# Windowed attention products over 64 keys, in one array shape of 64 rows by 32 columns

## The chip, the cores and the metric

The kernel runs on one core of one Trainium2 chip. The metric is the device time of one execution in microseconds (us), median of three runs. All times of instructions come from one profiled execution of the kernel before.

## What is computed

Eight batches of 512 tokens with 128 features are normalised, and two things are added to them: a global attention with 16 heads of width 8, and a stack of six layers. Each layer is a windowed attention followed by a gated feed-forward part. The windowed attention has 16 heads of width 64 and windows of 32 tokens; a query sees the 64 keys of its own window and of the one before it.

```
for i in range(DEPTH):                                     # 6 layers
    x = attn_layer(shift_tokens(x), Wqkv[i], q_scale[i], k_scale[i], Wo[i]) + x
    x = ffn_layer(shift_tokens(x), ln_g[i], ln_b[i], W1[i], b1[i], W2[i], b2[i]) + x
...
sim = jnp.einsum('bhwie,bhwje->bhwij', bq, bk2) * QK_SCALE # 32 queries x 64 keys, head width 64
sim = jnp.where(mask, -jnp.finfo(sim.dtype).max, sim)
attn = jax.nn.softmax(sim, -1)
out = jnp.einsum('bhwij,bhwje->bhwie', attn, bv2)
```

## The kernel before

Four blocks follow each other: the layer norm, the global attention, the windowed stack, and the final addition. The change concerns the windowed stack, `windowed_stack`, and the constants and buffers it takes from `Early`.

The stack works on 48 units, one for each layer and batch, of 512 tokens, which are four tiles of 128 tokens. Every engine runs a list of stages written out by hand (`PE_ORDER`, `DVE_ORDER`, `ACT_ORDER`, `POOL_ORDER`, `SP_ORDER`), again and again; a name such as `s2` is the stage `s` of tile 2, and a dash behind it says that it belongs to the unit before, so that two units overlap. Semaphores tie the stages together; nothing is reordered. TensorE's list, once a unit, is

```
q0 k0 qT3- kT3- r2- s3- vb2- k1 va2- kT0 q1 qT0 v0 r3- k2 va3- vb3- s0 q2 wo- qT1 r0 v1 kT1 centre- vb0 va0
var- q3 v2 s1 k3 qT2 h0- kT2 h1- r1 h2- s2 vb1 v3 va1 y-
```

`q`, `k`, `v` are the projections of a tile (line 1072); VectorE rotates q and k out of PSUM (`rotate_q`, `rotate_k`), ScalarE and GpSimd make the norms, VectorE scales (`scale_q`, `scale_k`), and TensorE transposes the result (`qT`, `kT`, line 1023), which ScalarE copies out. `s` makes the scores of a tile: two bf16 products lay the mask into both PSUM banks of a slot (line 1030), and 64 fp32 products of 32 queries by 64 keys are added to it (line 1041). VectorE takes the maximum and subtracts it, ScalarE takes the exponential (`exp`), `r` transposes the probabilities, ScalarE copies them to `probT`. `probT` holds in its 128 partitions the 64 keys of two windows, one above the other.

`va` and `vb` multiply the probabilities with the values (line 1053). Each of these stages has 16 fp32 products with 128 rows (two windows' keys) and 130 columns: the value buffers `va` and `vb` hold for each head two copies of 65 columns (64 values and a one, for the sum), of which one has zeros where the keys of the other window lie, so that one product gives both windows' results side by side. The second buffer, `vb`, holds the values shifted down by one window; the SyncE queue makes it from `va` with four DMAs a tile. ScalarE writes a tile of `va` with two copies of 64 partitions (lines 945 and 946). VectorE divides the results (lines 886 and 887) and transposes them (`turn`), and `wo` projects them (line 1095). `centre`, `var`, `h`, `y` are the feed-forward part.

PSUM is four slots of two banks. A stage on TensorE waits until the engine that read the stage before in its slot is done (`SLOTS_OF`). In TensorE's program the first four units are written out, then a loop goes over the rest, four units a turn; its head is aligned by `eng.addr_align(FETCH)`. A `passed` is a semaphore increment of the engine to itself; it stands behind some waits.

Of the kernel before, what the change touches and what calls it, by code (L numbers as in the profile page):

```python
# [6 lines left out]
BF16 = mybir.dt.bfloat16  # L7
# [33 lines left out]
class Early:  # L41

    def __init__(self, nc, ctx):
        sb = lambda n, s, d=F32: ctx.enter_context(nc.sbuf_tensor(n, s, d))
        sem = lambda n: ctx.enter_context(nc.semaphore(n))
        self.w_qkv = sb("w_qkv", [P, 2, 3, INNER])
        self.w_o = sb("w_o", [P, QCH, D])
        self.w_1 = sb("w_1", [P, 2, NJ, JW])
        self.w_2 = sb("w_2", [JW, NJ, D])
        self.b_1 = sb("b_1", [JW, 2, NJ])  # L50
        self.vec = sb("vec", [P, 3])
        self.qks = sb("qks", [P, 2, 2, DH])
        self.rot = sb("rot", [P, TPB, 4, DH])
        self.pair16 = sb("pair16", [P, 2, DH], BF16)
        self.mask = sb("mask", [P, 2, SEQ], BF16)
        self.ones = sb("ones", [P, P])
        self.centring = sb("centring", [P, P])
        self.zero = sb("zero", [P, 1])
        self.epsc = sb("epsc", [P, 1])
        self.least = sb("least", [P, 1])  # L60
        self.minus_least = sb("minus_least", [P, 1])
        self.xs = sb("xs", [P, SEQ])
        self.xs2 = sb("xs2", [P, SEQ])
        self.kT = [sb(f"kT{i}", [P, QCH, WIN + P]) for i in range(2)]
        self.va = sb("va", [P, VTILES, 2, HEADS, VA])
        self.vb = sb("vb", [P, VTILES, 2, HEADS, VA])
        self.S = {n: sem("ws_" + n) for n in ("const_loaded", "const_ready", "w_q", "w_k", "w_v", "qks_loaded", "w_ff",
                                              "cleared", "mask_loaded", "kept", "fetched")}

# [23 lines left out]
def layer_norm_and_transpose(nc, io, res, xT, ident, early):  # L93

    with ExitStack() as ctx:
# [30 lines left out]
        @block.gpsimd  # L126
        def _(pool):
            cleared, ready = early.S["cleared"], early.S["const_ready"]
            for k in early.kT:
                pool.memset(k[:, :, :], 0.0).then_inc(cleared, 1)  # L130
            for buffer, value in ((early.ones, 1.0 / D), (early.zero, 0.0), (early.epsc, EPS), (early.least, 1e-24),
                                  (early.minus_least, -1e-24), (early.xs, 0.0), (early.xs2, 0.0)):
                pool.memset(buffer[:, :], value).then_inc(cleared, 1)
            for v in (early.va, early.vb):
                pool.memset(v[:, :, :, :, :], 0.0).then_inc(cleared, 1)
            pool.wait_ge(cleared, 11)
            pool.wait_ge(loaded, 32)
            nc.gpsimd.tensor_tensor(early.centring[:, :], ident[:, :], early.ones[:, :], ALU.subtract).then_inc(cleared, 1)
            pool.wait_ge(cleared, 12)
            for v in (early.va, early.vb):  # L140
                pool.memset(v[0:DH, :, 0, :, DH:VA], 1.0).then_inc(ready, 1)
                pool.memset(v[DH:P, :, 1, :, DH:VA], 1.0).then_inc(ready, 1)

        @block.vector
        def _(dve):
# [22 lines left out]
        @block.scalar  # L168
        def _(act):
            act.wait_ge(agg_done, TILES + 1)  # L170
            nc.scalar.activation(std[:, :], std[:, :], ACT.Sqrt).then_inc(std_done, 1)
            for b in range(BATCH):
                act.wait_ge(transposed, b + 1)
                nc.scalar.copy(xT[:, b, :], ps[b % 2][:, :]).then_inc(moved, 1)
            act.wait_ge(early.S["mask_loaded"], 16)
            nc.scalar.copy(early.mask[:, :, :], mask32[:, :, :]).then_inc(early.S["const_ready"], 1)
            act.wait_ge(loaded, 32)
            for r in range(2):
                rows = slice(DH * r, DH * r + DH)
                nc.scalar.copy(early.pair16[rows, :, :], ident[rows, None, rows].broadcast_to([DH, 2, DH])).then_inc(  # L180
                    early.S["const_ready"], 1)

        @block.tensor
# [448 lines left out]
def windowed_stack(nc, io, xT, ident, early):  # L632
# [5 lines left out]
    with ExitStack() as ctx:  # L638
# [8 lines left out]
        qks = early.qks  # L647
        rot = early.rot
        table = sb("table", [P, TPB, 4, DH])
        pair16 = early.pair16  # L650
        mask = early.mask
        ones = early.ones
        centring = early.centring
# [32 lines left out]
                                                        "rstd_link", "passed"]}  # L686
        S.update(early.S)
        vb_ready = [sem(f"ws_vb_ready{t}") for t in range(TPB)]
        VB_DMAS = [3] + [4] * (TPB - 1)
        W_FF = 5  # L690
        CONSTS = 7
        block = ctx.enter_context(nc.Block())

        wait = event_wait(S, EVENTS)
# [59 lines left out]
        @block.sync  # L754
        def _(sp):
            for t in range(TPB):
                sp.sem_inc(vb_ready[t], 16 * VB_DMAS[t])
            def layer_end(it, l):

                for kind in "qkv":  # L760
                    wait(sp, kind + "_filled", it, 0)
                    passed(sp)
                sp.wait_ge(S["tables"], l + 1)
                passed(sp)
                early.load_qkv(sp, io, (l + 1) % DEPTH, (l + 1) % 2)
                if not isinstance(l, int):

                    wait(sp, "y_read", it - 1)
                    early.load_ff(sp, io, l)

            def stage(kind, t, unit, batch, before, starts, layer):

                s = t % VTILES
                wait(sp, "v_read", unit, t)
                sp.dma_start(vb[32:64, s, 0, :, :], va[0:32, s, 0, :, :]).then_inc(vb_ready[t], 16)
                sp.dma_start(vb[64:96, s, 1, :, :], va[32:64, s, 0, :, :]).then_inc(vb_ready[t], 16)
                sp.dma_start(vb[96:128, s, 1, :, :], va[64:96, s, 1, :, :]).then_inc(vb_ready[t], 16)
                if t:
                    sp.dma_start(vb[0:32, s, 0, :, :], va[96:128, (t - 1) % VTILES, 1, :, :]).then_inc(vb_ready[t], 16)
            units(sp, SP_ORDER, stage, layer_end)  # L780

            for name in ("w_q", "w_k", "w_v", "qks_loaded"):
                sp.wait_ge(S[name], 16 * (DEPTH + 1))
            for kind in "qkv":
                wait(sp, kind + "_filled", DEPTH * BATCH - 1, TPB - 1)
            early.fetch(sp, io)
# [21 lines left out]
        def _(dve):  # L808
# [39 lines left out]
            def stage(kind, n, unit, batch, before, starts, layer):  # L848
# [31 lines left out]
                elif kind in ("va", "vb"):  # L880
# [1 line left out]
                    wait(dve, kind + "_filled", unit, n)  # L882

                    wait_tile(dve, "turned", unit, n)
                    ps = slot(kind, n)[:, :, 0:4 * PITCH].rearrange("p r (w d) -> p r w d", d=PITCH)
                    link(nc.vector.reciprocal(rden[:, a], ps[:, :, :, DH]), kind)
                    nc.vector.tensor_tensor(o[:, a].rearrange("p w r d -> p r w d"), ps[:, :, :, 0:DH],  # L887
                                            rden[:, a, :, :, None].broadcast_to([P, 2, 4, DH]), ALU.mult).then_inc(S[kind + "_read"], 1)
                elif kind == "turn":

# [26 lines left out]
        def _(act):  # L917
# [9 lines left out]
            def stage(kind, n, unit, batch, before, starts, layer):  # L927
# [7 lines left out]
                elif kind == "v":  # L935
# [6 lines left out]
                        wait_vb(act, unit_of, old + 1)  # L942
                    wait(act, "v_filled", unit, n)
                    ps = flat("v", n).rearrange("p (h d) -> p h d", d=DH)
                    nc.scalar.copy(va[0:DH, n % VTILES, 0, :, 0:DH], ps[0:DH])  # L945
                    nc.scalar.copy(va[DH:P, n % VTILES, 1, :, 0:DH], ps[DH:P]).then_inc(S["v_read"], 1)
                elif kind == "qT":
                    wait(act, "qT_filled", unit, n)

# [67 lines left out]
        def _(pe):  # L1017
# [6 lines left out]
                return last  # L1024

            def scores(t):
                for r in range(2):
                    rows = slice(DH * r, DH * r + DH)

                    nc.tensor.matmul(slot("s", t)[:, r, :], pair16[rows, :, :].rearrange("p a n -> p (a n)"),  # L1030
                                     mask[rows, 0 if t == 0 else 1, :],
                                     start=True, stop=False, skip_group_check=True)
                for a in range(2):
                    for n, w in enumerate(WINDOWS):
                        tok = WIN * w
# [10 lines left out]

            def products(kind, t):
                a = ("va", "vb").index(kind)
                for r in range(2):
                    for n, values in enumerate((vb, va)):  # L1050
                        for g in range(4):

                            last = nc.tensor.matmul(  # L1053
                                slot(kind, t)[32 * g:32 * g + 32, r, 0:4 * PITCH].rearrange("p (w d) -> p w d", d=PITCH)[
                                    :, n::2, 0:VA],
                                probT[:, 4 * r + 2 * a + n, 32 * g:32 * g + 32],
                                values[:, t % VTILES, :, 2 * (4 * a + g) + r, :],
                                start=True, stop=True, skip_group_check=True)
                return last

            def stage(kind, n, unit, batch, before, starts, layer):
# [15 lines left out]
                elif kind == "s":  # L1077
                    wait(pe, "qT_read", unit, n)
                    wait(pe, "kT_read", unit, n)
                    last = scores(n)  # L1080
                elif kind == "r":
                    wait(pe, "probs", unit, n)
# [143 lines left out]
```

## Time and profile before

| | |
|---|---|
| median of three runs | 3814.31 us (3814.22 to 3814.42) |
| span of the profiled execution, first to last instruction | 3806.1 us |
| of it: layer norm and global attention | 473.5 us |
| of it: windowed stack and final addition, 48 units | 3332.6 us |
| mean granted TensorE clock | 0.984 of full speed |

The span is 8.2 us (0.2%) less than the median of the runs. Busy shares are those of the whole span. "PE" is TensorE's matrix products, "PEld" its weight loads, which run beside them. An fp32 product appears as two weight loads and two MATMULs, a bf16 product and a transpose as one of each.

### The profile page before, as it was taken

The numbers are of one execution on the slowest core, as the hardware profiler recorded it, in microseconds if no ns is written. First come the engines' busy times: TensorE is split into PE (matmuls) and PEld (weight loads), VectorE is DVE, ScalarE is ACT, GpSimd is POOL, SyncE is SP. The second block draws the span as 40 slices with busy tenths as digits, with TensorE's granted clock in tenths as the row PEclk, the third lists the DMA queues.
The fourth block names the chain that finished last, engine by engine and source line by source line (L and its number), as shares of the span: only waits on it lengthen the run. The fifth ranks groups of instructions, "written<-read, shape, count | busy, mean of one in ns | idle before, by whom it ended". The sixth has DMA issues, their size and how long they took to land. (4 is left out here: it accounts for less than half of the span.)

```text
span 3806.1 us, 123350 instructions
## 1 busy us (share of the span) xinstructions
PE 3546.5 (93%) x51360; PEld 2001.1 (53%) x51360; DVE 3233.6 (85%) x3696; ACT 2526.1 (66%) x3409; POOL 1558.0 (41%) x926
## 2 busy tenths in 40 slices
PE   5999879899999999999999999999999999999997
PEld 2333245555555555555555555555555555555554
DVE  7999778788888888888888888888888889888895
ACT  4888757667666666666766667667666666666764
POOL 4333144344434444434444434344444434444341
PEclk7999989999999999999999999999999999999999
DMA  2000011111121111121111111111211111211112
GB/s 69 2 1 1 23 44 34 28 27 34 29 61 34 27 34 28 37 58 27 34 28 34 50 38 34 28 29 38 55 34 29 27 40 27 62 29 27 37 30 62
DMA packets 60833, 130.63 MB, mean 34 GB/s; under 512 B 16004, under 2 KB 31880, under 8 KB 60424
## 3 DMA queue, kind: packets, MB, share of 16 engines
q1 hardware_dynamic: 60424, 124.06, 13.4%
q8 instruction: 393, 6.44, 0.7%
q14 instruction: 16, 0.13, 0.0%
HBM read 23.58 MB, written 4.19 MB: 7 GB/s over the span
## 5 line engine op out<-in xcount | busy, mean ns | idle before, releaser
L798 POOL TENSOR_TENSOR half_sq<-sq 128x1024 f32<-128x1024 f32 x192 | 500.9, 2609 | 1541.9 <-ACT sq L933 1531.9
L1072 PE MATMUL slot<-w_qkv,xs 128*128 (+1 forms) x2304 | 1102.7, 608 | 25.6 <-issue 17.3
L803 POOL TENSOR_TENSOR cosq<-cosq,sinq 128x1024 f32<-128x1024 f32 x384 | 902.2, 2366 | 368.7 <-DVE sinq L843 368.7
L933 ACT ACTIVATE sq<-slot 128x1024 f32<-128x1024 f32 x384 | 392.0, 1021 | 405.3 <-PE slot L1072 405.3
L1072 PEld LDWEIGHTS slot<-w_qkv,xs 128*128 128x128 f32 x2304 | 411.2, 192 | 432.2 <-issue 423.5
L841 DVE TENSOR_TENSOR cosq<-slot,table 128x1024 f32<-128x1024 f32 x384 | 467.7, 1218 | 143.4 <-ACT sq L933 133.1
L869 DVE TENSOR_TENSOR qk<-cosq,ry 128x1024 f32<-128x1024 f32 x384 | 517.8, 1359 | 11.6 <-ACT ry L990 9.5
L843 DVE TENSOR_TENSOR sinq<-slot,table 128x1024 f32<-128x1024 f32 x384 | 465.8, 1213 | 0.0
L1023 PEld LDWEIGHTS slot<-ident,qk 128*128 128x128 f32 x3072 | 349.5, 141 | 215.0 <-issue 125.3
L1023 PE MATMUL slot<-ident,qk 128*128 128x128 f32 x3072 | 396.1, 275 | 36.4 <-DVE qk L869 32.2
L1053 PE MATMUL slot<-vb,probT 128*32 128x130 f32 x6144 | 327.7, 280 | 16.9 <-issue 10.6
L1095 PE MATMUL slot<-oT,w_o 128*128 128x512 f32 x768 | 339.2, 595 | 2.4 <-DVE oT L894 2.4
L1041 PE MATMUL slot<-kT,qT 64*32 64x64 f32 x24576 | 296.2, 226 | 47.9 <-issue 47.3
L1053 PE MATMUL slot<-va,probT 128*32 128x130 f32 x6144 | 324.1, 276 | 14.6 <-issue 14.6
L455 DVE TENSOR_REDUCE at_rowmax<-at_slot 128x2 f32<-128x1024 f32 x256 | 303.9, 1219 | 14.6 <-PE at_slot L550 14.2
L1041 PEld LDWEIGHTS slot<-kT,qT 64*32 64x32 f32 x24576 | 258.2, 105 | 98.1 <-issue 97.7
L506 ACT ACTIVATE at_probs<-at_slot 128x1024 f32<-128x1024 f32 x256 | 255.9, 1027 | 71.3 <-PE at_slot L563 70.2
L877 DVE TENSOR_REDUCE smax<-slot 128x16 f32<-128x1024 f32 x192 | 233.8, 1218 | 71.3 <-PE slot L1041 69.6
L945 ACT COPY va<-slot 64x1024 f32<-64x1024 f32 x192 | 192.5, 1002 | 147.4 <-PE slot L1053 126.4
L887 DVE TENSOR_TENSOR o<-slot,rden 128x512 f32<-128x512 f32 x384 | 265.4, 691 | 13.2
L1106 PE MATMUL slot<-xs,w 128*114 128x512 f32 x576 | 272.1, 596 | 3.1 <-ACT xs L1002 3.1
L1053 PEld LDWEIGHTS slot<-vb,probT 128*32 128x32 f32 x6144 | 167.0, 109 | 177.7 <-issue 172.4
(123 smaller groups left out, 4940.6 us busy)
## 6 DMA issues: line engine op xcount, KB each, us to landing
vb<-va SPq DMA_DIRECT2D x720, 130.0 KB, 2.3
w_qkv<-in_w_qkv SPq DMA_DIRECT2D x21, 512.0 KB, 5.3
w_o<-in_w_o SPq DMA_DIRECT2D x6, 512.0 KB
w<-in_w SPq DMA_DIRECT2D x6, 342.0 KB
res<-in_x SPq DMA_DIRECT2D x4, 512.0 KB, 5.3
out<-w_qkv SPq DMA_DIRECT2D x8, 256.0 KB, 3.2
kept<-res SPq DMA_DIRECT2D x1, 1536.0 KB, 6.2
w<-in_w SPq DMA_DIRECT2D x6, 171.0 KB
```

The costliest lines, as they stand in the source:

```text
L455: nc.vector.reduce_max(rowmax[:, :, n], slot("max", n)[:, :, :], AX.X).then_inc(S["max_read"], 1)
L798: nc.gpsimd.tensor_tensor(half_sq[:, :, :], squares[:, :, 0, :], squares[:, :, 1, :], ALU.add).then_inc(S["folded"], 1)
L803: nc.gpsimd.tensor_tensor(cosq[:, side], cosq[:, side], sinq[:, side], ALU.add).then_inc(S["qk"[side] + "_added"], 1)
L841: nc.vector.tensor_tensor(cosq[:, side].rearrange("p h a d -> p h (a d)"), ps.rearrange("p h a d -> p h (a d)"), cos[:, None, :].broadcast ...
L843: nc.vector.tensor_tensor(sinq[:, side], ps[:, :, ::-1, :], sin.rearrange("p (a d) -> p a d", a=2)[:, None, :, :].broadcast_to([P, HEADS, ...
L869: nc.vector.tensor_tensor(qk[:, side], cosq[:, side].rearrange("p h a d -> p h (a d)"), ry[:, side * HEADS:(side + 1) * HEADS, None].broad ...
L933: nc.scalar.activation(sq[:, "qk".index(name)].rearrange("p h d -> p (h d)"), flat(name, n), ACT.Square).then_inc(S[name + "_squared"], 1)
L1023: last = nc.tensor.transpose(flat(kind, n)[:, c * P:(c + 1) * P], src[:, c * P:(c + 1) * P], ident[:, :])
L1041: last = nc.tensor.matmul(slot("s", t)[32 * g:32 * g + 32, r, (4 * a + n) * DH:(4 * a + n + 1) * DH], qT[rows, c, tok:tok + WIN], kT[t % 2 ...
L1053: last = nc.tensor.matmul(slot(kind, t)[32 * g:32 * g + 32, r, 0:4 * PITCH].rearrange("p (w d) -> p w d", d=PITCH)[:, n::2, 0:VA], probT[: ...
L1072: last = nc.tensor.matmul(slot(kind, n)[:, i, :], xs[:, n * P:(n + 1) * P], w_qkv[:, (0 if layer is None else layer) % 2, "qkv".index(kind ...
L1095: last = nc.tensor.matmul(slot("wo")[:, 0, :], w_o[:, c, :], oT[:, :, a, :, r, half, :], start=c == 0, stop=c == QCH - 1)
```

## The change

Two things are changed in the array's use. The products with the values no longer run over 128 rows against padded values. Each is cut into two, one for each 64 rows (the keys of one window), with 65 columns, and the two write to the two banks of the slot. The padding copies in `va` and `vb` go away, so the buffers are half as large, ScalarE writes a tile of `va` in one copy of 128 partitions, and two DMAs a tile replace four (of the same bytes). And the mask is laid by eight bf16 products of 32 columns of weights (4 column groups by 2 row halves) where there were two of 128. The scores' products, which were in the shape 64 x 32 already, stay. A `passed` is added behind the waits of `s`.

```diff
@@ Early, layer_norm_and_transpose
-        self.pair16 = sb("pair16", [P, 2, DH], BF16)
+        self.unit16 = sb("unit16", [P, WIN], BF16)
...
-        self.va = sb("va", [P, VTILES, 2, HEADS, VA])
-        self.vb = sb("vb", [P, VTILES, 2, HEADS, VA])
+        self.va = sb("va", [P, VTILES, HEADS, VA])
+        self.vb = sb("vb", [P, VTILES, HEADS, VA])
...
-                nc.scalar.copy(early.pair16[rows, :, :], ident[rows, None, rows].broadcast_to([DH, 2, DH])).then_inc(
+                nc.scalar.copy(early.unit16[rows, :], ident[rows, DH * r:DH * r + WIN]).then_inc(
@@ SyncE, stage vb
-                sp.dma_start(vb[32:64, s, 0, :, :], va[0:32, s, 0, :, :]).then_inc(vb_ready[t], 16)
-                sp.dma_start(vb[64:96, s, 1, :, :], va[32:64, s, 0, :, :]).then_inc(vb_ready[t], 16)
-                sp.dma_start(vb[96:128, s, 1, :, :], va[64:96, s, 1, :, :]).then_inc(vb_ready[t], 16)
+                sp.dma_start(vb[32:128, s, :, :], va[0:96, s, :, :]).then_inc(vb_ready[t], 16)
                 if t:
-                    sp.dma_start(vb[0:32, s, 0, :, :], va[96:128, (t - 1) % VTILES, 1, :, :]).then_inc(vb_ready[t], 16)
+                    sp.dma_start(vb[0:32, s, :, :], va[96:128, (t - 1) % VTILES, :, :]).then_inc(vb_ready[t], 16)
@@ ScalarE, stage v
-                    nc.scalar.copy(va[0:DH, n % VTILES, 0, :, 0:DH], ps[0:DH])
-                    nc.scalar.copy(va[DH:P, n % VTILES, 1, :, 0:DH], ps[DH:P]).then_inc(S["v_read"], 1)
+                    nc.scalar.copy(va[:, n % VTILES, :, 0:DH], ps).then_inc(S["v_read"], 1)
@@ TensorE, scores
-                for r in range(2):
-                    rows = slice(DH * r, DH * r + DH)
-
-                    nc.tensor.matmul(slot("s", t)[:, r, :], pair16[rows, :, :].rearrange("p a n -> p (a n)"),
-                                     mask[rows, 0 if t == 0 else 1, :],
-                                     start=True, stop=False, skip_group_check=True)
+                for g in range(4):
+                    for r in range(2):
+                        rows = slice(DH * r, DH * r + DH)
+
+                        nc.tensor.matmul(slot("s", t)[32 * g:32 * g + 32, r, :], unit16[rows, :],
+                                         mask[rows, 0 if t == 0 else 1, :],
+                                         start=True, stop=False, skip_group_check=True)
@@ TensorE, products
-                for r in range(2):
-                    for n, values in enumerate((vb, va)):
+                for n, values in enumerate((vb, va)):
+                    for r in range(2):
+                        at = (2 * n + r) * PITCH
                         for g in range(4):
-
-                            last = nc.tensor.matmul(
-                                slot(kind, t)[32 * g:32 * g + 32, r, 0:4 * PITCH].rearrange("p (w d) -> p w d", d=PITCH)[
-                                    :, n::2, 0:VA],
-                                probT[:, 4 * r + 2 * a + n, 32 * g:32 * g + 32],
-                                values[:, t % VTILES, :, 2 * (4 * a + g) + r, :],
-                                start=True, stop=True, skip_group_check=True)
+                            for b in range(2):
+                                keys = slice(DH * b, DH * b + DH)
+
+                                last = nc.tensor.matmul(
+                                    slot(kind, t)[32 * g:32 * g + 32, b, at:at + VA],
+                                    probT[keys, 4 * r + 2 * a + n, 32 * g:32 * g + 32],
+                                    values[keys, t % VTILES, 2 * (4 * a + g) + r, :],
+                                    start=True, stop=True, skip_group_check=True)
@@ TensorE, stage s
                     wait(pe, "kT_read", unit, n)
+                    passed(pe)
                     last = scores(n)
```

The two places that matter are in TensorE's program. The first is the end of the run `va3- vb3- s0`, with `q2` behind it: slot0 takes the results of `vb3`, slot1 the scores. Before:

```order
L1053 MATMUL slot0<-vb,probT 32x2x65 [waits ws_vb_ready3,ws_q_read,ws_r_read]
L1053 MATMUL slot0<-vb,probT 32x2x65 x3
L1053 MATMUL slot0<-va,probT 32x2x65 x4
L1053 MATMUL slot0<-vb,probT 32x2x65 x4
L1053 MATMUL slot0<-va,probT 32x2x65 x4
L1030 MATMUL slot1<-mask,pair16 128x512 [waits ws_kT_read,ws_qT_read,ws_va_read]
L1030 MATMUL slot1<-mask,pair16 128x512
L1041 MATMUL slot1<-kT0,qT 32x64 x64
L1072 MATMUL slot0<-w_qkv,xs 128x512 [waits ws_vb_read]
```

and in the changed kernel, whose line numbers differ a little:

```order
L1053 MATMUL slot0<-vb,probT 32x65 [waits ws_vb_ready3,ws_q_read,ws_r_read]
L1053 MATMUL slot0<-vb,probT 32x65 x15
L1053 MATMUL slot0<-va,probT 32x65 x16
L1027 MATMUL slot1<-mask,unit16 32x512 [waits ws_kT_read,ws_va_read,ws_qT_read]
L1027 MATMUL slot1<-mask,unit16 32x512 x7
L1038 MATMUL slot1<-kT0,qT 32x64 x64
L1071 MATMUL slot0<-w_qkv,xs 128x512 [waits ws_vb_read]
```

The waits stand where they stood; each products stage has 32 products in place of 16, and the mask 8 in place of 2. The second place is the run `s3- vb2- k1 va2-`, in which the scores' products and the values' products follow each other directly (slot0 and slot2 take the results). Before:

```order
L1030 MATMUL slot1<-mask,pair16 128x512 [waits ws_kT_read,ws_qT_read]
L1030 MATMUL slot1<-mask,pair16 128x512
L1041 MATMUL slot1<-kT1,qT 32x64 x64
L1053 MATMUL slot0<-vb,probT 32x2x65 [waits ws_vb_ready2,ws_r_read]
L1053 MATMUL slot0<-vb,probT 32x2x65 x3
```

and in the changed kernel:

```order
L1027 MATMUL slot1<-mask,unit16 32x512 [waits ws_kT_read,ws_qT_read]
L1027 MATMUL slot1<-mask,unit16 32x512 x7
L1038 MATMUL slot1<-kT1,qT 32x64 x64
L1053 MATMUL slot0<-vb,probT 32x65 [waits ws_vb_ready2,ws_r_read]
L1053 MATMUL slot0<-vb,probT 32x65 x15
```

No stage has moved against another on any engine.

## Rows read from the trace of the kernel before

**Rows 1.** The page's first part: busy time, share of the span, instructions of each engine.

```profile
span 3806.1 us, 123350 instructions
PE 3546.5 (93%) x51360; PEld 2001.1 (53%) x51360; DVE 3233.6 (85%) x3696; ACT 2526.1 (66%) x3409; POOL 1558.0 (41%) x926
```

**Rows 2.** Busy time by stretch, for four units (from one q0 to the next).

```profile
core 0: us, PE busy (x) PEld busy (x) DVE busy (x) ACT busy (x) POOL busy (x), PEclk, DMA share, GB/s
2110.70:2177.80 67.10, 64.65 (x958) 38.34 (x959) 59.17 (x68) 44.80 (x62) 29.16 (x12) 1.00 0.14 31
2177.80:2251.60 73.80, 66.98 (x960) 39.47 (x959) 58.25 (x63) 45.40 (x63) 29.09 (x12) 0.95 0.24 65
...
sum 275.10, PE 261.22 PEld 154.27 DVE 235.83 ACT 181.93 POOL 116.52; mean PE 65.30 PEld 38.57 DVE 58.96 ACT 45.48 POOL 29.13
```

**Rows 3.** Groups by line, whole span: TensorE's value products, scores and mask.

```profile
L1053 PE MATMUL slot<-vb,probT 128*32 128x130 f32 x6144 | 327.7, 280 | 16.9 <-issue 10.6 <-ACT probT L968 1.2 <-ACT kT L959 0.4
L1041 PE MATMUL slot<-kT,qT 64*32 64x64 f32 x24576 | 296.2, 226 | 47.9 <-issue 47.3
```

**Rows 4.** Timeline of TensorE, `va3- vb3- s0 q2`: start, duration, group, idle before.

```profile
2132.24 0.43 PE L1053 MATMUL slot<-vb,probT 128*32 128x130 f32 x8
...
2133.16 0.40 PE L1053 MATMUL slot<-vb,probT 128*32 128x130 f32 x8
...
2134.40 0.39 PE L1030 MATMUL slot<-mask,pair 64*128 64x512 bf16 x2 [0.17 <-DVE o L887]
2134.72 1.48 PE L1041 MATMUL slot<-kT,qT 64*32 64x64 f32 x128
2136.13 1.99 PE L1072 MATMUL slot<-w_qkv,xs 128*128 x4
```

**Rows 5.** Timeline of VectorE, its stage `va3-` in the same place.

```profile
2133.41 0.21 DVE L886 RECIPROCAL rden<-slot 128x8 f32<-128x8 f32 x1 [0.73 <-PE slot L1053]
```

**Rows 6.** Timeline of TensorE, `va2-` and `kT0`, 10 us earlier.

```profile
2122.45 0.43 PE L1053 MATMUL slot<-vb,probT 128*32 128x130 f32 x8
...
2124.35 1.07 PE L1023 MATMUL slot<-ident,qk 128*128 128x128 f32 x8 [0.80 <-DVE qk L869]
```

**Rows 7.** Timeline of TensorE, `s2 vb1 v3 va1` of the next unit.

```profile
2242.11 1.49 PE L1041 MATMUL slot<-kT,qT 64*32 64x64 f32 x128
2243.69 0.43 PE L1053 MATMUL slot<-vb,probT 128*32 128x130 f32 x8
...
2245.38 0.31 PE L1053 MATMUL slot<-vb,probT 128*32 128x130 f32 x3 [0.86 <-issue]
...
2247.87 0.43 PE L1053 MATMUL slot<-vb,probT 128*32 128x130 f32 x8
...
2248.89 2.84 PE L1110 MATMUL slot<-hid,w 114*128 114x512 f32 x6
```

**Rows 8.** Timeline of TensorE: two gaps, in `s2` and in the next `s3-`.

```profile
2170.68 0.35 PE L1041 MATMUL slot<-kT,qT 64*32 64x64 f32 x16 [0.83 <-issue]
...
2185.06 1.43 PE L1041 MATMUL slot<-kT,qT 64*32 64x64 f32 x122
2191.63 0.43 PE L1041 MATMUL slot<-kT,qT 64*32 64x64 f32 x6 [5.13 <-issue]
```

**Rows 9.** The page's third part: the DMA queue that brings instructions.

```profile
q8 instruction: 393, 6.44, 0.7%
```

**Rows 10.** Waits of TensorE from 1020 to 3742 us, 40 units: total, times, longest.

```profile
PE slot L1041 <- issue: 40.9, 28, 5.1
PE slot L1053 <- issue: 19.5, 23, 1.4
PE slot L1023 <- DVE qk L869: 18.4, 20, 1.0
...
PE slot L1072 <- issue: 9.6, 10, 1.2
```

**Rows 11.** Groups by line, whole span: the first of ScalarE's two copies of a tile of values.

```profile
L945 ACT COPY va<-slot 64x1024 f32<-64x1024 f32 x192 | 192.5, 1002 | 147.4 <-PE slot L1053 126.4 <-PE slot L1072 21.0
```

More of the change, by code:

```diff
@@ L134, in _ @@
             for v in (early.va, early.vb):
-                pool.memset(v[:, :, :, :, :], 0.0).then_inc(cleared, 1)
+                pool.memset(v[:, :, :, :], 0.0).then_inc(cleared, 1)
             pool.wait_ge(cleared, 11)
@@ L140, in _ @@
             for v in (early.va, early.vb):
-                pool.memset(v[0:DH, :, 0, :, DH:VA], 1.0).then_inc(ready, 1)
-                pool.memset(v[DH:P, :, 1, :, DH:VA], 1.0).then_inc(ready, 1)
+                pool.memset(v[:, :, :, DH:VA], 1.0).then_inc(ready, 1)
         @block.vector
@@ L649, in windowed_stack @@
         table = sb("table", [P, TPB, 4, DH])
-        pair16 = early.pair16
+        unit16 = early.unit16
         mask = early.mask
@@ L688, in windowed_stack @@
         vb_ready = [sem(f"ws_vb_ready{t}") for t in range(TPB)]
-        VB_DMAS = [3] + [4] * (TPB - 1)
+        VB_DMAS = [1] + [2] * (TPB - 1)
         W_FF = 5
-        CONSTS = 7
+        CONSTS = 5
         block = ctx.enter_context(nc.Block())
@@ L884, in stage @@
                     wait_tile(dve, "turned", unit, n)
-                    ps = slot(kind, n)[:, :, 0:4 * PITCH].rearrange("p r (w d) -> p r w d", d=PITCH)
+                    ps = slot(kind, n)[:, :, 0:4 * PITCH].rearrange("p b (x d) -> p b x d", d=PITCH)
                     link(nc.vector.reciprocal(rden[:, a], ps[:, :, :, DH]), kind)
-                    nc.vector.tensor_tensor(o[:, a].rearrange("p w r d -> p r w d"), ps[:, :, :, 0:DH],
+                    nc.vector.tensor_tensor(o[:, a].rearrange("p (b w) r d -> p b (w r) d", b=2), ps[:, :, :, 0:DH],
                                             rden[:, a, :, :, None].broadcast_to([P, 2, 4, DH]), ALU.mult).then_inc(S[kind + "_read"], 1)
```

## The prediction

> **What bounds the kernel now.** I read the page first: TensorE is busy 93% of the span, VectorE 85%, ScalarE 66% [rows 1]. Then the busy times of each unit of the stack. Four units take 275.1 us, and TensorE is busy in 261.2 of them; one unit takes 67.1 us, the next 73.8 us, with the same instructions [rows 2]. So TensorE sets the pace, and something that isn't work costs several us now and then.
>
> The list of TensorE's waits says what: most of its idle time is "issue", that is, it waits for nothing that the profile shows. It sits inside the scores (40.9 us in 40 units), inside the value products (19.5 us) and at the loop's head (9.6 us) [rows 10]. That is 70 us in ten turns of the loop, 7.0 us a turn of four units. The timeline shows where. A gap of 0.83 us lies in the middle of `s2`, the next one, 5.13 us, in the middle of `s3-` of the next unit [rows 8]. Between the ends of these two the timeline has 246 MATMULs of TensorE (16 of scores, 32 of `vb1`, 4, 32 of `va1`, 6, 8, 24 of transposes, 2 of mask, 122 of scores), so 492 instructions with their weight loads, and some 20 on semaphores: 512. The queue that brings instructions moved 6.44 MB in 393 packets, 16.4 kB each [rows 9]. I read this as: the program comes in blocks of 256 instructions, and a gap opens at a block's border when the block before it was used up before the next one had come. For a block that TensorE used up fast I count from the trace: the one that ends at 2245.38 began with the 22nd pair of `s2`, at about 2242.25, and holds 2.0 us of work, a gap and 128 pairs; it took 3.1 us [rows 7]. With the mean gap in the products (19.5 / 23 = 0.85 us) in place of its own it would be 2.85, with the longest, 1.4 us, 3.4 [rows 10]. I take 3.0 us as the least time for a block, and 2.8 and 3.4 as ends. The 5.13 us fall where the weights of the next layers are being loaded (65 GB/s in that unit against 31 [rows 2]), which holds up the block's transfer; weights are loaded once in eight units, so in every other turn.
>
> The other thing that TensorE waits for is VectorE, in two places of a unit: `kT0` for `scale_k`, up to 1.0 us where no gap came just before [rows 6, 10], and `s0`, whose slot VectorE must have read, 0.17 us [rows 4]. From q0 to kT0 VectorE's chain (square, two rotations, norms, softmax of `s3-`, scale) is the bound; in the rest of the unit VectorE waits for TensorE (0.73 us ahead of `va3-` [rows 5]).
>
> **The change, part by part.** *Value products.* A stage of 32 MATMULs takes 0.92 us when another follows in the same shape (2132.24 to 2133.16 [rows 4]) and 1.02 us to the start of another shape (2247.87 to 2248.89 [rows 7]). Afterwards it has 64 MATMULs in the shape of the scores, of 65 columns in place of 64. The scores' 128 MATMULs take 1.41 us to the next stage's start (2134.72 to 2136.13 [rows 4]), 11 ns each. The last one's own 0.2 us (226 ns each [rows 3]) doesn't halve, so 64 take (1.41 - 0.2)/2 + 0.2 = 0.80 us, or a little less, since the first are the fastest: I take 0.78, with 0.70 (half) and 1.02 (nothing won) as ends. What counts of it in a unit:
> `va1` and `vb1`, 0.24 us each; `va3-` 0.22 us; `vb0 va0` together 0.30 us (the semaphore instructions between them are no longer hidden behind slow products). `vb3-` gives nothing: `s0` waits for VectorE's reading of `va3-`, which takes from 2133.41 to 2134.40, 0.99 us, whatever `vb3-` takes [rows 4, 5]. `vb2-` and `va2-` give nothing, since `kT0` already waits for VectorE behind them [rows 6]. Sum 1.00 us.
>
> *Mask.* It takes 0.32 us until the scores start [rows 4], of which part is the change of shape. Afterwards there is no change of shape, but eight pairs in place of two. Ends: nothing won, and 0.22 us won. I take 0.15 us for `s0`, `s1`, `s2`, 0.45 us; `s3-` lies in VectorE's stretch.
>
> *The added `passed`* is a semaphore instruction behind the waits of `s`. Before `s1` and `s2` the queue has long products to hide it; before `s0`, where TensorE waits anyway, it may be in the open: 0 to 0.1 us, I take 0.05. What stands behind it is s0, then q2 and wo, on which VectorE's residual waits.
>
> *ScalarE's copies.* Two copies of 1.0 us become one [rows 11]: 4 us less of 45 us a unit. No stage of TensorE or VectorE waits for them now (`v_read` is early), so 0. The DMAs carry the same bytes with two fewer issues a tile on SP's queue, whose results are wanted over 10 us later: 0. Without that cover they would cost their landing time of some 2 us.
>
> So TensorE's path gets shorter by 1.00 + 0.45 - 0.05 = 1.40 us a unit, 67 us in 48 units.
>
> *Instructions.* Each value stage has 32 pairs more, eight stages a unit; each mask six more, four a unit: 280 pairs, 560 instructions, with the `passed` 564. I counted the loop in program order: 7,905 instructions before, 10,161 afterwards, which is 39.7 blocks. A unit is 9.92 blocks, so the borders fall in nearly the same place in every unit. Beginning with the head of the loop, these blocks hold little time:
> the one that begins in `va3-` and ends in the scores of `s0` (four times a turn): the rest of `va3-` and `vb3-` with the wait for VectorE, then mask and scores, about 2.05 us, 0.95 us short of 3.0;
> the one that begins in the scores of `s2` and ends in `vb1` (four times): 1.0 + 0.3 + 0.3 = 1.6 us, 1.4 us short;
> one that is all `vb0 va0` (once): 1.5 us, 1.5 us short;
> at the loading of weights, in VectorE's stretch: the wait of 1.0 us at `kT0` and the 0.5 us that `vb2-` and `va2-` give up are free there, and the block holds 1.0 us more work than the one before did; of a gap like the long one 5.1 - 1.5 - 1.0 = 2.6 us are left, in every other turn: 1.3 us on average;
> the loop's head, 1.0 us as before.
> Sum: 3.8 + 5.6 + 1.5 + 1.3 + 1.0 = 13.2 us a turn. Before it was 7.0 us, and 0.6 for the lower clock after the long gap (0.95 in that unit [rows 2]), 7.6. So 5.6 us more in each of 12 times four units, 67 us.
>
> The two cancel. The span of the profiled execution, 3806.1 us [rows 1], stays, and so does the median of the runs, 8.2 us over it: **3814 us**.
>
> The Trainium skill, "Runtime: NRT & Kernel Launch", "Instruction fetch mechanics", says that instructions come in blocks of 16 KiB (256 instructions) by the sequencer's own queue, and that crossing a border is mostly hidden since dispatch is slower than the fill. The block's size agrees with [rows 9]; that it is hidden doesn't, with 5.1 us in one gap [rows 8]. By its word the new gaps would not come, and only the 67 us would be left.
>
> **The rivals.** (a) *The gaps stay as they are, faster.* Speaking for it: most blocks are slow, and of the 31 a turn only a handful gave gaps. Against it: all blocks of which I know that they held about 2 us of work gave one. Then the gain stands alone: 3814 - 67 = 3747, and with the best ends of mask and product stages (below) 3722. Chance 0.13.
> (b) *The cancellation, within 1%*: chance 0.52. Its ends come from the unknown prices: the block's least time of 2.8 or 3.4 us moves nine gaps a turn by 0.2 or 0.4 us, 22 or 43 us; the mask's ends, three times a unit, 10 or 22 us; a product stage of 0.70 in place of 0.78 us gives 15 us. Together 3814 - 47 = 3767 to 3814 + 65 = 3879, and both ends at once are rarer than one: 3772 to 3860.
> (c) *The gap in `s0` and the one in `vb1` cost more than they should, slower.* If the value buffers' DMAs hold up the transfer of every second of the nine short blocks of a turn, by as much as the longest gap in the products (1.4 us [rows 10]), that is 6.3 us a turn and 76 us, 3889; if of every fourth, 3851. Held up by over 0.1 us each, they make the kernel slower. Chance 0.2.
> (d) *The products of 64 rows don't run eight at a time, slower.* If each half costs half of the old one (two at 14 ns for 28), the stages last 0.92 us as before, and only the mask gains (19 us); the gaps grow by some 4.2 us a turn in place of 5.6, as the blocks hold 0.15 us more work: 3814 - 19 + 50 = 3845. Against it: the scores in the same shape run at 11 ns [rows 4]. Chance 0.12.
> (e) *A floor for each product, much slower.* If a product couldn't start within 25 ns of another, a stage of 64 would take 1.6 us, 0.7 us more than now, 8 times in each of 48 units, over 250 us: about 4070. The scores' 11 ns [rows 4] speak against it: chance 0.03. The Trainium skill has this floor of 25 ns in "TensorE: Matmul & The Clock Gate", "Wait — 56ns, not 53.3ns?", and this case's trace doesn't agree for products in different tiles of the array.
>
> **How the numbers follow.** The likeliest is (b), 3814 us. Range 3752 to 3865: it holds (b), the half of (c) and (d), and leaves out (a) to a large part and (e). What can be told from no change is about 0.2%, 8 us. Of (b) a little under half lies on the faster side (0.20), 0.20 within, 0.12 and less on the slower side, since the mask and the first fast pairs may give more than I took; with (a) faster 0.40; with (c), (d), (e) slower 0.40; within 0.20.
>
> **What would show it.** The scores' and products' MATMULs at 10 to 11 ns from start to start, a single products stage of 0.75 to 0.8 us: if 0.9, (d). "Issue" waits of TensorE at the products and scores near 12 us a turn of four units, in `s0` and in `vb1` in every unit: if 6, (a). Units of nearly equal length, without the 5 us gap. The wait of `kT0` for VectorE grown to over 1 us. What would make me wrong is a block's least time other than 3.0 us, or the gaps' falling where TensorE waits anyway.

## The result, and the profile after

The changed kernel takes 3925.73 us (median of 4 runs, 3924.01 to 3941.89) against 3814.26 us before (median of 4): 1.030 times, with a 95% interval of 1.0287 to 1.0320. I had said 3814 with a range to 3865. It is slower by 111 us, outside the range.

The page's first part, and the queue that brings instructions, of the kernel after:

```profile
span 3925.1 us, 149905 instructions
PE 3493.3 (89%) x64800; PEld 1975.0 (50%) x64800; DVE 3218.1 (82%) x3696; ACT 2330.8 (59%) x3217; POOL 1551.9 (40%) x924
...
q8 instruction: 501, 8.21, 0.9%
```

Against [rows 1], every engine is busy for a shorter time, TensorE by 53 us and ScalarE by 195, and yet the span is longer by 119. So no busy time was added. TensorE's waits, in the ten turns of the loop between 1020 and 3860 us (total, times, longest):

```profile
PE slot L1038 <- issue: 99.6, 63, 5.1
PE slot L1053 <- issue: 84.2, 64, 2.0
PE slot L1019 <- DVE qk L866: 24.7, 20, 1.5
PE slot L1027 <- ACT kT L955: 17.5, 40, 0.5
PE slot L1071 <- issue: 13.3, 10, 1.7
```

Here is the time. "Issue" inside the scores (L1038), the value products (L1053) and at the loop's head (L1071) was 7.0 us a turn of four units [rows 10]; it is (99.6 + 84.2 + 13.3) / 10 = 19.7 us now. A turn takes 281.9 us in place of 272.7 (ten turns: 2818.9 and 2726.7 us).

One unit of the timeline of TensorE, with rows left out between its places (`s3- vb2-`; `vb3- s0`; `vb0 va0 var-`; `vb1 v3 va1 y-`):

```profile
2104.33 0.41 PE L1027 MATMUL slot<-mask,unit 64*32 64x512 bf16 x8 [0.44 <-ACT kT L955]
2104.55 1.31 PE L1038 MATMUL slot<-kT,qT 64*32 64x64 f32 x110
2107.66 0.38 PE L1038 MATMUL slot<-kT,qT 64*32 64x64 f32 x18 [1.80 <-issue]
...
2121.91 0.41 PE L1027 MATMUL slot<-mask,unit 64*32 64x512 bf16 x8 [0.22 <-DVE o L884]
2122.13 0.75 PE L1038 MATMUL slot<-kT,qT 64*32 64x64 f32 x54
2123.73 0.99 PE L1038 MATMUL slot<-kT,qT 64*32 64x64 f32 x74 [0.86 <-issue]
...
2157.97 0.41 PE L1027 MATMUL slot<-mask,unit 64*32 64x512 bf16 x8
2158.20 1.46 PE L1038 MATMUL slot<-kT,qT 64*32 64x64 f32 x128
...
2161.81 0.34 PE L1053 MATMUL slot<-va,probT 64*32 64x65 f32 x12 [1.24 <-issue]
...
2163.99 0.46 PE L1053 MATMUL slot<-vb,probT 64*32 64x65 f32 x32
...
2164.78 2.84 PE L1110 MATMUL slot<-hid,w 114*128 114x512 f32 x6
```

and one row of the next unit but one, `s3-` while the weights of the next layers are being loaded:

```profile
2249.33 0.89 PE L1038 MATMUL slot<-kT,qT 64*32 64x64 f32 x39 [4.76 <-issue]
```

The reader is to see the gaps (1.80 us in `s3-`, 0.86 in `s0`, 1.24 in `vb1`, and the 4.76 us), and that the products themselves got faster: `va1`, 64 MATMULs, takes 2163.99 to 2164.78, 0.79 us, where it took 1.02 [rows 7], and the mask 0.23 us (2157.97 to 2158.20) where it took 0.32 [rows 4].

The lower clock has a smaller share. Two rows from another unit, a gap in `vb1` and the projection `v3` behind it, and the busy times of that stretch beside an undisturbed one (stretch, then us busy of each engine, then the granted clock):

```profile
1103.08 0.28 PE L1053 MATMUL slot<-vb,probT 64*32 64x65 f32 x6 [1.55 <-issue]
...
1103.70 3.42 PE L1071 MATMUL slot<-w_qkv,xs 128*128 x4
```

```profile
1103.70:1107.10 3.40, 3.40 (x17) 1.02 (x16) 1.76 (x3) 0.00 (x0) 0.00 (x0) 0.56 0.02 5
2108.70:2110.60 1.90, 1.90 (x14) 0.68 (x4) 1.86 (x3) 0.00 (x0) 1.04 (x1) 1.00 0.03 9
```

After 1.55 us of idle time the granted clock is 0.56, so mostly at 1.2 GHz, and four MATMULs take 3.42 us where four of the same take 1.99 [rows 4]. Most gaps were not followed by this: of 98 "issue" waits of over 1 us between 1020 and 3860 us, the clock fell to its lower level in or just behind 21, for 85.0 us in all; in the kernel before it was there for 30.6 us between 1020 and 3742 us. Over the whole execution the mean clock is 0.972 against 0.984 before.

### The profile page after: what moved, and what is told of

Read it like the earlier page. It is cut to its first block and busy times, and to the rows that moved or that the text cites. A ratio compares the mean times of both kernels' runs of the same rounds, so it can differ in the third digit from the quotient of the medians.

```text
span 3925.1 us, 149905 instructions
## 1 busy us (share of the span) xinstructions
PE 3493.3 (89%) x64800; PEld 1975.0 (50%) x64800; DVE 3218.1 (82%) x3696; ACT 2330.8 (59%) x3217; POOL 1551.9 (40%) x924
## 5 line engine op out<-in xcount | busy, mean ns | idle before, releaser
L1071 PE MATMUL slot<-w_qkv,xs 128*128 (+1 forms) x2304 | 1127.9, 620 | 34.6 <-issue 25.9
L1071 PEld LDWEIGHTS slot<-w_qkv,xs 128*128 128x128 f32 x2304 | 417.5, 195 | 439.8 <-issue 414.6
L866 DVE TENSOR_TENSOR qk<-cosq,ry 128x1024 f32<-128x1024 f32 x384 | 505.5, 1327 | 62.3 <-ACT ry L986 61.0
L1038 PE MATMUL slot<-kT,qT 64*32 64x64 f32 x24576 | 300.3, 225 | 117.6 <-issue 117.6
L1038 PEld LDWEIGHTS slot<-kT,qT 64*32 64x32 f32 x24576 | 285.6, 105 | 137.9 <-issue 129.5
L1053 PE MATMUL slot<-va,probT 64*32 64x65 f32 x12288 | 243.8, 230 | 57.4 <-issue 57.3
L942 ACT COPY va<-slot 128x1024 f32<-128x1024 f32 x192 | 193.7, 1009 | 147.5 <-PE slot L1053 110.6
L884 DVE TENSOR_TENSOR o<-slot,rden 128x512 f32<-128x512 f32 x384 | 265.5, 691 | 13.3
L954 ACT COPY kT<-slot 128x1024 f32<-128x1024 f32 x192 | 194.4, 1013 | 96.1 <-PE slot L1019 96.1
L1053 PEld LDWEIGHTS slot<-vb,probT 64*32 64x32 f32 x12288 | 128.0, 108 | 230.0 <-issue 223.5
```

The costliest lines, as they stand in the source:

```text
L866: nc.vector.tensor_tensor(qk[:, side], cosq[:, side].rearrange("p h a d -> p h (a d)"), ry[:, side * HEADS:(side + 1) * HEADS, None].broad ...
L1038: last = nc.tensor.matmul(slot("s", t)[32 * g:32 * g + 32, r, (4 * a + n) * DH:(4 * a + n + 1) * DH], qT[rows, c, tok:tok + WIN], kT[t % 2 ...
L1053: last = nc.tensor.matmul(slot(kind, t)[32 * g:32 * g + 32, b, at:at + VA], probT[keys, 4 * r + 2 * a + n, 32 * g:32 * g + 32], values[key ...
L1071: last = nc.tensor.matmul(slot(kind, n)[:, i, :], xs[:, n * P:(n + 1) * P], w_qkv[:, (0 if layer is None else layer) % 2, "qkv".index(kind ...
```

## The experiments

Thirteen kernels' figures, the two given ones among them. Median; length of a turn; "issue" waits of TensorE a turn (their sum between 1050 and 3650 us by the turns in it); instructions a turn.

Kernels were timed in four groups, each beside runs of the kernel before on the same chip (medians of 3814.6 to 3818.7 us); the ratios in the text are to those. The turns and waits come from one profiled execution each, which can differ from the median (3936.9 us for products_only, 3898.0 for after_swap, 3812.9 for before_40, 3800.9 for mask_only_40).

| kernel | median us | turn us | issue us a turn | instructions |
|---|---|---|---|---|
| before | 3814.3 | 272.7 | 7.2 | 7,905 |
| before_40 | 3801.9 | 272.4 | 7.4 | 7,905 |
| mask_only | 3832.3 | 273.6 | 8.1 | 8,113 |
| mask_only_176 | 3875.2 | 278.4 | 13.0 | 8,113 |
| mask_only_40 | 3788.6 | 270.7 | 5.6 | 8,113 |
| products_only | 3924.2 | 283.3 | 18.8 | 9,969 |
| after | 3925.7 | 281.9 | 19.5 | 10,161 |
| after_small | 3918.7 | 281.9 | 18.8 | 10,161 |
| after_32 | 3888.5 | 277.9 | 15.2 | 10,161 |
| after_swap | 3883.0 | 279.5 | 16.1 | 10,161 |
| after_swap_32 | 3839.9 | 273.1 | 12.3 | 10,161 |
| after_bf16 | 3777.8 | 269.2 | 15.7 | 8,113 |
| before_bf16 | 3718.5 | 265.6 | 7.5 | 6,881 |

A fourteenth, filled, stands below.

**One part alone.** mask_only is the kernel before with these lines of the change: `unit16`, the eight mask products, and the `passed` ahead of `scores`.

```diff
-                    nc.tensor.matmul(slot("s", t)[:, r, :], pair16[rows, :, :].rearrange("p a n -> p (a n)"),
+                        nc.tensor.matmul(slot("s", t)[32 * g:32 * g + 32, r, :], unit16[rows, :],
...
+                    passed(pe)
```

> [...] Supply theory (the time went to gaps at the borders of 256-instruction blocks): a loop turn of 8,113 instructions, its borders moved; counted from the trace of before, with a least time of 3.3 us for a block, the short blocks of a turn miss 1.6 us in place of 5.2. With the mask's own 0.12 to 0.15 us three times a unit (18 to 22 us in all): 3750 to 3796 us. Rival, the eight mask products are themselves the cost: over 3830 us, with the time from s_read or kT_read to the first score longer than before's 0.32 us. If the gaps stay as they were: 3794.

products_only is the kernel after with the mask put back.

> The kernel after with before's mask of two products: the 64-row value products, their buffers and copies alone. Supply theory: 9,969 instructions a turn, blocks missing 14 us a turn as in the kernel after (13.8 by the same count), without the mask's 18 to 22 us: 3925 to 3950 us. If the mask part is what cost the time: about 3814. If the products' gain and the gaps cancelled as I forecast: 3830.

Measured: 3832.3 (ratio 1.0058, 1.0032 to 1.0083) and 3924.2 us (1.0272, 1.0236 to 1.0307). The value products carry nearly all of the loss. mask_only missed its range by 36 us: the short blocks that I had counted went, but others came late. Its 3832.3 us would also fit the rival "over 3830 us", but not the rival's other sign: from the first mask product to the first score it takes 0.22 us each time, where it took 0.32. The mask's work got cheaper, by somewhat less than I had thought: the turn is 0.9 us longer with 2.2 us more idle time of every kind in it, so 1.3 us of work less, 0.33 a unit.

**The same instructions at another address.** The edit is one number, which moves the loop against the borders of the blocks and executes nothing:

```diff
-                eng.addr_align(FETCH)
+                eng.addr_align(FETCH, offset=176)
```

> The same instructions as mask_only; only the address at which the loop begins lies 176 instruction slots past a block's border in place of 0. Supply theory: the borders now fall so that some ten blocks of a turn hold under 2 us of work; from the same count, 16.4 us a turn missing against 1.6 (12.8 against 0.8 with a least time of 3.0 us); of some of these VectorE's stretch hides a part. 80 to 175 us slower than mask_only: 3850 to 3950 us. Any theory in which the products' own time, the DMAs, ScalarE or the semaphores decide: the same time as mask_only within 8 us.

> The same instructions as mask_only, the loop beginning 40 slots past a block's border. From the trace of mask_only: short blocks would miss 3 us a turn in place of 1.6, but blocks that begin with a wait (counted at 3.2 us after their 64th instruction) 11.6 in place of 17.3. If both theories of a late block hold (short blocks, and waits early in a block), 2 to 4 us a turn less: 3785 to 3815 us, at or under the kernel before. If only short blocks counted: some 15 us slower than mask_only, 3845 us.

> The kernel before, the same instructions, only the loop beginning 40 slots past a block's border as in mask_only_40: how much of that kernel's 0.8% is the place of the borders and how much the mask. From the trace of before: short blocks miss 6 to 7 us a turn in place of 5, blocks that begin with a wait 15 in place of 16, so no clear change: 3800 to 3835 us, and the mask of eight products is then worth its 16 to 22 us where the borders allow it. Rival, the move alone makes any such loop faster: 3785 to 3795 us, and the mask is worth nothing.

Measured: 3875.2 at 176 (1.0155, 1.0137 to 1.0174), 3832.3 at 0, 3788.6 at 40 (0.9923, 0.9909 to 0.9936), with TensorE's "issue" waits between 1050 and 3650 us, for the three in this order:

```profile
PE slot L1054 <- issue: 79.3, 64, 5.0
PE slot L1042 <- issue: 32.8, 33, 2.4
...
PE slot L1073 <- issue: 9.0, 9, 1.2
```

```profile
PE slot L1042 <- issue: 68.1, 53, 5.9
...
PE slot L1073 <- issue: 7.2, 9, 1.1
...
PE slot L1054 <- issue: 1.4, 6, 0.3
```

```profile
PE slot L1042 <- issue: 22.9, 23, 2.3
PE slot L1073 <- issue: 17.4, 19, 1.2
...
PE slot L1054 <- issue: 13.2, 19, 2.5
```

87 us lie between the slowest and the fastest of three kernels with the same instructions, and the gaps move from the products (L1054) to the scores (L1042) with the address. That settles what kind of thing the gaps are. The traces show it a second way, by the gaps' places. Number TensorE's instructions in order of their start from the loop's branch, add the offset, and take the remainder by 256. Of the 105 "issue" waits in ten turns of mask_only_176 that are not at the loop's head, 95 come to 31 or 32; of the 62 in mask_only all but 6; in mask_only_40 the long ones too (42.9 of 46.4 us). In the changed kernel 125 of 126 come to 11 or 12. The gaps stand at the borders of blocks of 256 instructions and move with them.

The size I had expected from 0 to 176 (80 to 175) was too large, 43 us. before_40 takes 3801.9 us (0.9957, 0.9939 to 0.9976), within its range: the move alone is worth 0.4% there, and the mask at the same place another 0.3%, some 13 us where I had put 16 to 22. Both steps are small against the spread of the executions (3787.6 to 3813.0 us for before_40), and the kept trace of before_40 has no fewer gaps than that of before (7.4 us a turn), so what its 0.4% comes from is not shown.

**More instructions, the same products.** Behind each value product stands one of a single column into a column that nobody reads, ahead of the mask six more.

```diff
+                            last = nc.tensor.matmul(
+                                slot(kind, t)[32 * g:32 * g + 32, r, 4 * PITCH:4 * PITCH + 1],
+                                probT[:, 4 * r + 2 * a + n, 32 * g:32 * g + 32],
+                                values[:, t % VTILES, 0, 2 * (4 * a + g) + r, 0:1],
```

> The kernel before, its products and mask unchanged, with as many more instructions as the kernel after has, in the same stages: behind each value product one of a single column into a column that nobody reads, ahead of the mask six one-column products, and the passed. Supply theory: TensorE's gaps without a reason in the profile grow from 7.0 us a turn to 11 or more, at the same places as in the kernel after (the scores of s0, vb1 in every unit); with the fillers' own work of 0.5 to 1.5 us a unit (24 to 72 us): 3880 to 3960 us. Rival, a count of instructions costs nothing: gaps stay at 7.0 us a turn, 3838 to 3886 us from the fillers' work alone.

Measured: 4031.7 us, over the range. The "issue" waits rose to 123.8 us in the same window, 13.8 us a turn; a turn takes 290.7 us, so of its 18.0 us more the gaps are 6.6 and the rest 2.9 us a unit, the fillers' own work less what TensorE no longer waits for others, about twice what I allowed. It shows that the count brings the gaps without the new products; as a measure of their price it is too coarse.

**What makes the block in `s3-` late.** I had two theories: the copies from `va` to `vb`, now in two bursts, hold up the block; or it is asked for late. In the unit shown above the block's packet can be found: between 2102.8, where TensorE crossed a border, and 2105.2 us no packet moved on any queue; between 2105.2 and 2106.5 there was one, this:

```profile
q8 instruction: 1, 0.02, 5.5%
```

It started 0.9 us after TensorE had got past its wait for kT (2104.33), it was there by 2106.4, and the first instruction of it ran at 2107.66. after_small cuts the bytes:

```diff
-                sp.dma_start(vb[32:128, s, :, :], va[0:96, s, :, :]).then_inc(vb_ready[t], 16)
+                sp.dma_start(vb[32:128, s, 0:1, :], va[0:96, s, 0:1, :]).then_inc(vb_ready[t], 16)
```

> The kernel after, with the copies from va to vb cut to one head of sixteen (a sixteenth of the bytes; the other heads of vb keep their first values, so the windows' earlier keys are left out of those heads' values). Theory A, the copies' packets hold up the transfer of instruction blocks: the gaps of about 2.2 us in the scores of s3- vanish, TensorE's unexplained waits at the scores fall from 10.0 us a turn to about 5, the time to about 3870 us. Theory B, a block's transfer is asked for only about 1.1 us after TensorE's queue has passed a wait that stands early in the block before: the gaps in s3- stay, 3915 to 3935 us.

after_32 moves the borders:

```diff
+                eng.addr_align(FETCH, offset=32)
```

> The kernel after, the same instructions, only the loop begins 32 slots past a block's border. The borders fall 32 instructions earlier in the program, so that the waits of s3- stand at 70 to 90 in their block in two of four units in place of 38 to 59. Theory B: in these units the next block is asked for before the wait, and the gap in s3- goes; the short blocks miss 13.6 us a turn in place of 13.8, so of the gaps some 2 to 4 us a turn go: 3875 to 3905 us. Theory A, or gaps that depend on the transfers alone: 3920 to 3930 us.

after_small takes 3918.7 us (1.0263, 1.0246 to 1.0280), and its gap in `s3-` stands at the same place of the unit and is as long; after_small first, then the kernel after:

```profile
2031.54 0.45 PE L1038 MATMUL slot<-kT,qT 64*32 64x64 f32 x28 [1.90 <-issue]
```

```profile
2036.73 0.45 PE L1038 MATMUL slot<-kT,qT 64*32 64x64 f32 x28 [1.90 <-issue]
```

after_32 takes 3888.5 us (1.0187, 1.0170 to 1.0204), and its waits in the scores fall to 53.4 us from 92.7:

```profile
PE slot L1053 <- issue: 67.2, 56, 2.2
PE slot L1038 <- issue: 53.4, 45, 2.6
```

In ten turns the gaps in `s3-` come to 18.2 us, in one unit of four, in place of 58.7 in three, as theory B had it; shorter new ones stand in the first unit, 1.7 us a turn in `va2-` and 1.0 in `wo`. So the copies are not what makes the block late, and both runs came out as theory B said. It isn't the whole rule: in mask_only a block with a wait near its head was asked for at once in some turns and after the wait in others (1.1 us behind its border in one turn, 5.3 to 5.9 in six), and I can't say what decides.

**Work put into the short block.**

```diff
-    "var- q3 v2 s1 k3 qT2 h0- kT2 h1- r1 h2- s2 vb1 v3 va1 y- ")
+    "var- q3 v2 s1 k3 qT2 h0- kT2 h1- r1 h2- s2 v3 vb1 va1 y- ")
```

> The kernel after with v3 ahead of vb1 in TensorE's order (s2 v3 vb1 va1 in place of s2 vb1 v3 va1). The block that ends in vb1 then holds 1.9 us of projection more. Theory (supply): the gap of 1.2 to 2.2 us in vb1 of every unit goes to 0 to 0.4 us; VectorE gets vb1 1.9 us later less the gap, which its slack may or may not cover. 6 us a turn of gaps less, so 3850 to 3880 us; if VectorE has to wait for vb1 and hands it on, up to 3920 us. If the gap were something of the products themselves: no less idle time at the products, 3926 us or more.

> after_swap and after_32 together: the whole change, v3 ahead of vb1, the loop 32 slots past a border. The two moves take away different gaps (vb1's, and part of those in s3-): 37 and 43 us add to 3846 us; 3835 to 3885 us with the lower clock that the swap brought. Not under the kernel before.

Measured: 3883.0 (1.0166, 1.0149 to 1.0183) and 3839.9 us (1.0067, 1.0052 to 1.0082); the first is 3 us over the range of the theory. Timeline of after_swap, `s2 v3 vb1`:

```profile
2067.47 1.46 PE L1038 MATMUL slot<-kT,qT 64*32 64x64 f32 x128
2068.88 1.98 PE L1071 MATMUL slot<-w_qkv,xs 128*128 x4
2070.79 0.46 PE L1053 MATMUL slot<-vb,probT 64*32 64x65 f32 x32
2071.06 0.85 PE L1053 MATMUL slot<-va,probT 64*32 64x65 f32 x32
```

The gap in `vb1` is gone, and the products' "issue" waits with it (14.2 us in the window, from 75.3). Part went elsewhere: the scores' waits rose to 113.7 from 92.7, and the granted clock fell to 0.961 from 0.972.

**Half the instructions of the products.** In after_bf16 and before_bf16 `probT`, `va` and `vb` are bf16, so values and probabilities are rounded; that is all of the edit.

```diff
-        probT = sb("probT", [P, 8, P])
+        probT = sb("probT", [P, 8, P], BF16)
```

> The kernel after with probT, va and vb in bf16 (so the values and probabilities are rounded): each value product takes one pair of instructions in place of two, 512 instructions less in a unit, 8,113 in a turn, which is mask_only's count; half the bytes in the copies. Supply theory: the products' work shrinks by another 0.35 us where it counts, and blocks missing 4 us a turn in place of 14: 3730 to 3790 us, faster than before. If it was the 64-row form or its buffers that cost the time, not the count: over 3850 us.

> The kernel before with probT, va and vb in bf16 (values and probabilities rounded), its 128-row products as they were: 16 MATMULs a stage in place of 32, 256 instructions less in a unit, some 6,881 in a turn. Supply theory: the count decides, so this beats the 64-row form in bf16 (3778 us, 8,113 instructions a turn): a products stage from 0.92 to about 0.55 us, four times a unit, is 1.5 us a unit or 71 us, and blocks missing 3.9 us a turn by the count of short blocks in place of 5.2: 3700 to 3765 us. Rival, the 64-row form is the faster one once products take a single pass: 3780 us or more.

Measured: 3777.8 (0.9909, 0.9887 to 0.9932) and 3718.5 us (0.9748, 0.9727 to 0.9769). Both medians are as expected, but for after_bf16 partly by luck: its gaps are 15.7 us a turn, not 4, and the work shrank by more than I had counted. The comparison of the two stands: with a single pass as with two, the 128-row form with half the instructions is faster, here by 59 us, and again the difference in gaps (8.2 us a turn) is larger than that of the turns (3.6). Whether the 64-row form would lead if no block came late is argued from that, not shown.

## Why the prediction was wrong

*The gain* of 1.40 us a unit, 5.6 a turn, was right in its pieces and isn't contradicted by the sum. A products stage between other stages takes 0.79 us in the median where it took 1.02 (0.78 forecast), `vb0 va0` together 1.56 where they took 1.91, the mask 0.22 where it took 0.32 (0.15 us of gain forecast, 0.1 measured). The forecast had left out what VectorE takes back, so it is to be held against a turn less its "issue" waits: 272.7 - 7.0 = 265.7 us before and 281.9 - 19.7 = 262.2 after, 3.5 us less. The lower clock hides part of the gain. Between 1050 and 3650 us the mean granted clock is 0.985 against 0.994, which by my estimate is at most 0.015 x 281.9 - 0.006 x 272.7 = 2.6 us a turn. I had counted on the opposite, 0.6 us a turn won back.

*The gaps* were the step that failed, "Sum: 3.8 + 5.6 + 1.5 + 1.3 + 1.0 = 13.2 us a turn". It is 19.7: in the scores 10.0 where I had 5.1 (3.8 + 1.3), in the products 8.4 for 7.1, at the head 1.3 for 1.0. By place, summed over ten turns of the trace and given a turn: `s0` 4.1 us (forecast 3.8), `vb1` 6.3 (5.6), `vb0 va0` 1.3 (1.5), `s3-` 5.9 (1.3), the head 1.3 (1.0), and 0.6 in `va2-`, which I had at nothing. So the places with short blocks all had their gap in every turn, at nearly the forecast size, and the term that failed is the one for `s3-`.

*The term for `s3-`.* I counted only blocks with little time in them. The three blocks of a turn that end in `s3-` last longer, two of them 5.3 to 6.8 us and one 9.1 to 12.1 (with their gap), and are late all the same, since they are asked for late: in the unit shown, and by after_32, behind a wait. The gap is 1.8 to 2.4 us where it comes late (17 times in ten turns), and 4.2 to 5.1 in the five turns in which weights are being loaded. I had put 1.3 us a turn for the latter, taking [rows 8]'s long gap as the old one less what other work would cover, and nothing for the others. That is 4.6 of the 6.5 us a turn. Nor is it the transfer that the weights hold up, as I had written: in these five turns the packet starts 8.7 to 9.7 us behind the border in place of 6.6 to 6.8, and then takes 0.9 to 1.0 us.

*The least time of a block*, 3.0 us, was too small, and that it cost little was luck. The ninety late short blocks of ten turns lasted 2.8 to 4.0 us, 3.4 on average, 0.4 us more in each of nine. But they also held more work than I had counted (`vb1`'s 3.4 - 1.6 = 1.8 us for 1.6, `vb0 va0` 2.2 for 1.5), so the gaps grew by 0.8 us a turn only. The trace of before could have told me: of the 3.1 us of the block in [rows 7] only 0.86 is gap, which leaves 2.3 us of work and not 2.0, and the ends would have been 3.1 and 3.7 in place of 2.8 and 3.4. In these late blocks the packet starts 0.5 to 1.6 us behind the border and takes 0.9 to 1.4 us, and the first instruction starts 1.2 to 1.6 us after the packet's end.

*Rival (c)*, slower by gaps that cost more than they should (3851 to 3889), had the right direction with the wrong cause and the wrong places: the value buffers' copies don't hold up blocks (after_small, 7 us). The chances were added up wrongly too: those of the rivals come to 0.33 for faster and 0.47 for slower, not 0.40 each. Rivals (d) and (e) are out by the stage's 0.79 us. Rival (a) is out by the "issue" rows. That ScalarE's shorter copy and the fewer issues are worth 0 is as forecast: nobody waits for them now either. `passed` wasn't tried by itself; what it can cost lies within mask_only's account. The kT0 wait for VectorE grew to 1.2 us on average (24.7 / 20), as said.

*What stays open*: when a block is asked for at once and when behind a wait; and why the packet starts 2 to 3 us later while weights are being loaded.

## What to carry to other kernels

Where many small matmuls stand together, count instructions as well as array time: here the blocks of 256 that held about 2 us of work each cost a gap of 1.0 to 1.8 us on average, and a form that halves a product and doubles its pairs can lose more at the borders of the blocks than it wins in the array. Before a change of the instruction count is judged, try the loop at two or three offsets, since the same instructions differed by 2.3% here; mask_only_40 beats the kernel before by 0.8% with the same arithmetic, and before_bf16 by 2.5% where bf16 values are allowed. A wait near a block's head may delay the next block, so a long block is no proof of a fed sequencer.

## What I had not expected of the hardware

The next block's packet came 0.9 us behind a wait that TensorE had sat in (2104.33 to 2105.2 us), with all queues empty meanwhile; I had thought of the transfer as started by the border. And a gap can cost twice: behind one of 1.55 us the granted clock read 0.56 for 3.4 us, and a projection took 3.42 us in place of 1.98. The Trainium skill, "Runtime: NRT & Kernel Launch", "Instruction fetch mechanics", has the crossing of a block's border mostly hidden. The trace agrees for some two thirds of the borders (13.7 "issue" waits a turn in 39.7 blocks) and not for the others, which cost 19.7 us a turn, 7% of it.
